# Forward row transform on sums and differences of the two image halves, with transposes, in a spectral convolution kernel

## What is computed

```python
    # layer 1
    m = jnp.mean(g, axis=(2, 3, 4), keepdims=True); s = jnp.var(...)   # _gn, groups of two channels
    x_ft = jnp.fft.rfft2(x)
    top = jnp.einsum('bixy,ioxy->boxy', x_ft[:, :, :m1, :m2], w1)      # m1 = m2 = 32
    bot = jnp.einsum('bixy,ioxy->boxy', x_ft[:, :, -m1:, :m2], w2)
    ...
    return jnp.fft.irfft2(out_ft, s=(h, w))
```

## Time and profile before

| | us |
|---|---|
| median of 3 runs | 2803.64 (2803.63 to 2803.73) |
| profiled execution | 2809.89 |
| its span (first to last instruction) | 2808.1 |
| PE busy in the span | 2221.9 (79%) |
| DVE busy | 1756.9 (63%) |
| ACT busy | 1290.3 (46%) |
| POOL busy | 554.7 (20%) |

### The profile page before, as it was taken

The page is one execution under the profiler, slowest core; times in us unless marked ns, Lnnn a source line. Parts: engine busy times, 40 slices in busy tenths (PEclk is TensorE's granted clock), DMA queues, the critical chain, the costliest instruction groups (busy, mean ns, idle before and its releaser), DMA issues. The chain is left out here.

```text
span 2808.1 us, 37222 instructions
## 1 busy us (share of the span) xinstructions
PE 2221.9 (79%) x15026; PEld 1346.0 (48%) x15026; DVE 1756.9 (63%) x1704; ACT 1290.3 (46%) x1562; POOL 554.7 (20%) x427
## 2 busy tenths in 40 slices
PE   0000089999999999998999999956676999888894
PEld 0000033333333333328999999955665555444452
DVE  8999889999999999992333333320001666545452
ACT  1111178889888898875445555510001222211110
POOL 1000024555333346330000000000100222111121
PEclk9999999999999999998999999988898999999997
DMA  9999869999999999978667777749998999999999
GB/s 403 431 430 418 320 219 342 342 340 347 332 335 347 335 347 343 340 247 325 234 256 258 263 254 264 265 135 388 395 395 320 372 417 417 418 417 417 418 417 387
DMA packets 419767, 958.23 MB, mean 341 GB/s; under 512 B 13888, under 2 KB 325744, under 8 KB 375312
## 3 DMA queue, kind: packets, MB, share of 16 engines
q1 hardware_dynamic: 230192, 593.46, 56.7%
q0 software_dynamic: 52176, 201.95, 18.0%
q10 hardware_dynamic: 137232, 160.45, 16.8%
HBM read 662.20 MB, written 293.60 MB: 340 GB/s over the span
## 5 line engine op out<-in xcount | busy, mean ns | idle before, releaser
L471 PE MATMUL psum<-mix_u,wcur 128*64 128x512 f32 x2048 | 881.9, 592 | 5.4 <-DVE mix_u L565 4.9
L471 PE MATMUL psum<-mix_v,wcur 128*64 128x512 f32 x2048 | 881.9, 592 | 0.0
L471 PEld LDWEIGHTS psum<-mix_u,wcur 128*64 128x64 f32 x2048 | 277.3, 136 | 596.1 <-issue 571.7
L1185 PE MATMUL psum<-tab_irow_icol,inv_t 128*128 128x512 f32 x1024 | 490.2, 602 | 50.0 <-ACT inv_t L1241 45.4
L1286 DVE TENSOR_TENSOR weights_or_rows<-weights_or_rows,psum 128x1024 f32<-128x1024 f32 x224 | 273.2, 1221 | 194.1 <-PE psum L1185 182.2
L1024 DVE COPY fwd_cols<-psum 128x544 f32<-128x544 f32 x128 | 141.8, 1108 | 396.8 <-PE psum L818 396.8
L818 PE MATMUL psum<-tab_frow_fcol_both_ident,fwd_x 128*128 128x128 f32 x3072 | 352.4, 276 | 4.2 <-DMA fwd_x<-x_scratch 4.2
L818 PEld LDWEIGHTS psum<-tab_frow_fcol_both_ident,fwd_x 128*128 128x128 f32 x3072 | 348.5, 193 | 5.5 <-DMA fwd_x<-x_scratch 4.3
L383 POOL COPY mix_v<-mix_u 64x2321 f32<-64x2321 f32 x128 | 339.4, 2652 | 26.6 <-PE psum L471 18.7
L729 DVE SCALAR_TENSOR_TENSOR tiles<-tiles 128x2048 f32<-128x2048 f32 x128 | 322.2, 2518 | 4.0
L510 ACT ACTIVATE tiles<-tiles,pcur 128x2048 f32<-128x2048 f32 x128 | 268.1, 2095 | 111.7 <-DVE tiles L729 105.1
(11 more groups left out here) (187 smaller groups left out, 1631.9 us busy)
## 6 DMA issues: line engine op xcount, KB each, us to landing
mix_u<-x SPq DMA_DIRECT2D x120, 1280.0 KB, 9.4
tiles<-x SPq DMA_DIRECT2D x64, 2048.0 KB, 12.4
x_scratch<-tiles ACTq DMA_DIRECT2D x128, 1024.0 KB, 9.2
weights_or_rows<-x_scratch SPq DMA_DIRECT2D x112, 1024.0 KB, 11.8
out<-weights_or_rows POOLq DMA_DIRECT2D x112, 1024.0 KB, 42.3
fwd_x<-x_scratch SPq DMA_DIRECT2D x96, 1024.0 KB, 6.8
x_tile<-x_scratch SPq DMA_DIRECT2D x46, 1024.0 KB, 9.0
weights_or_rows<-L_conv_w_real POOLq DMA_DIRECT2D x8, 4096.0 KB, 22.2
```

What stands on the lines that cost most here:

```text
L471: last = nc.tensor.matmul(bank(k * 4 + q, 512, C, e * C), wcur[j][:, e, m * C:(m + 1) * C], taps[e][:, r0:r0 + 2, m:m + W], start=(m == 0) ...
L1185: last = nc.tensor.matmul(bank(n % 2 * 2 + a), TS[n % 2][:, a * P:(a + 1) * P], icol, start=True, stop=True)
```

## The change

Rows 0 to 127 and 128 to 255 of the image are folded first. For an even mode the second half has the same table as the first, for an odd one the negated table. So the even modes need only the sum of the halves and the odd ones only the difference. `DVE` makes the sums (`sums_of`, 4 channels, 1024 elements), `POOL` the differences, each into four buffers. `frow` becomes two tables of 64 columns: cosines and sines of 17 even or 16 odd modes.

`rows(n)` now handles 2 channels, with the table as the stationary operand (64 columns) and the image as the moving one (512 columns); even modes go to partitions 0 to 63 and odd ones to 64 to 127 of one bank. The modes now lie on the partitions. ACT (even n) and DVE (odd n) copy a bank into `RS`, and PE turns it with four transposes of 128x128, so that the image column is on the partitions again. `turned` copies two such results at once with two DVE copies into `A`, which is laid out [column half a, parity, channel, 34]. Its innermost index is the mode, so `columns` reads its stationary operand with a stride of 34 floats. Four banks hold rows, two the transposes, and two are left for the columns (four before). ACT's squares share one scratch buffer, so each waits for the last. A tile's buffer is free again after sums, differences and squares, no longer after the rows. A step u of the new order handles 4 channels: two `rows`, two `transposes`. There are 16 steps per batch; column parts come after steps 1, 3, 5, 7 and 9.

```diff
-    frow = np.zeros((P, 2, P))
-    for half in range(2):
-        a = th * np.outer(np.arange(P) + half * P, np.arange(NM))
-        frow[:, half, :NM] = np.cos(a)
-        frow[:, half, NM2:NM2 + NM] = np.sin(a)
+    frow = np.zeros((P, 2, C))
+    for par in range(2):
+        k = np.arange(par, NM, 2)
+        a = th * np.outer(np.arange(P), k)
+        frow[:, par, :len(k)] = np.cos(a)
+        frow[:, par, NP:NP + len(k)] = np.sin(a)
...
-            A = [sb(ph, f"fwd_cols{i}", [P, 2, 4 * NP, C]) for i in range(2)]
+            ED = [[sb(ph, f"fwd_{n}{i}", [P, CG // 2, W]) for n in ("sum", "diff")] for i in range(NE)]
+            RS = [sb(ph, f"fwd_rows{i}", [P, 512]) for i in range(4)]
+            A = [sb(ph, f"fwd_cols{i}", [P, 2, 2, C, 2 * NP]) for i in range(2)]
...
-            junk = [sb(ph, f"fwd_junk{i}", [P, 2, 2 * W]) for i in range(2)]
+            junk = [sb(ph, f"fwd_junk{i}", [P, 2, 2 * W]) for i in range(1)]
...
+                    def rows(n):
+
+                        if n % 2 == 0:
+                            pe.wait_ge(sums_done, n // 2 + 1)
+                            pe.wait_ge(diff_done, n // 2 + 1)
+
+                        if n >= 4:
+                            pe.wait_ge(row_dve if n % 2 else row_act, (n - 4) // 2 + 1)
+                        for par in range(2):
+                            last = nc.tensor.matmul(bank(n % 4, 512, C, par * C), frow[:, par, :],
+                                                    ED[n // 2 % NE][par][:, n % 2 * 2:n % 2 * 2 + 2, :],
+                                                    start=True, stop=True)
                         last.then_inc(row_done, 1)
+
+                    def transposes(n):
+
+                        pe.wait_ge(row_dve if n % 2 else row_act, n // 2 + 1)
+                        if n == 0:
+                            pe.wait_ge(n2, 4)
+                        if n >= 2:
+                            pe.wait_ge(tr_out, n // 2 * 2)
+                        for q in range(4):
+                            at = (4 + n % 2) * 512 + q * P
+                            last = nc.tensor.transpose(psum[:, at:at + P], RS[n % 4][:, q * P:(q + 1) * P], ident)
+                        last.then_inc(tr_done, 1)
...
-                                mode = k * 2 * NP + 2 * p
                                 last = nc.tensor.matmul(
                                     psum[0:pair * C, at:at + P],
-                                    A[c % 2][:, a, mode:mode + pair, :].rearrange("p m c -> p (m c)"),
+                                    A[c % 2][:, a, 0:pair, :, k * NP + p].rearrange("p m c -> p (m c)"),
                                     fcol[:, a, k, :], start=(q == 0), stop=(q == 3))
...
+                    rows(0)
+                    rows(1)
+                    for u in range(NU_):
+                        c, g, second = u // 16 - 1, u % 16 // 2, u % 2 == 1
+                        if u + 1 < NU_:
+                            rows(2 * u + 2)
+                            rows(2 * u + 3)
+                        transposes(2 * u)
+                        transposes(2 * u + 1)
+                        if c >= 0 and g == 0 and not second:
+                            norm(c)
+                        if c >= 0 and second and g < PARTS:
+                            columns(c, g)
...
-                            if k >= 2:
-                                act.wait_ge(sq_done, k - 1)
-                            nc.scalar.activation(junk[g % 2][:, :, :],
+                            if k >= 1:
+                                act.wait_ge(sq_done, k)
+                            nc.scalar.activation(junk[0][:, :, :],
...
+                    def row_copy(n):
+
+                        dve.wait_ge(row_done, n + 1)
+                        if n >= 4:
+                            dve.wait_ge(tr_done, n - 3)
+                        v.tensor_copy(RS[n % 4][:, :], bank(n % 4)).then_inc(row_dve, 1)
+
+                    def turned(u):
+
+                        c, c0 = u // 16, u % 16 * 4
+                        if u % 16 == 0 and c >= 2:
+                            dve.wait_ge(col_done, (c - 1) * PARTS)
+                        dve.wait_ge(tr_done, 2 * u + 2)
+                        src = psum[:, 2048:3072].rearrange("p (c a r m) -> p c a r m", c=4, a=2, r=2)
+                        for a in range(2):
+                            dst = A[c % 2][:, a, :, c0:c0 + 4, :].rearrange("p r c m -> p c r m")
+                            last = v.tensor_copy(dst, src[:, :, a, :, 0:2 * NP])
+                        last.then_inc(tr_out, 2)
...
+                @block.gpsimd
+                def _(pool):
+                    for h in range(2 * B * NG):
+                        t = h // 2
+                        pool.wait_ge(loaded[t % NX], loaded_by(t))
+                        if h >= NE:
+                            pool.wait_ge(row_done, 2 * (h - NE) + 2)
+                        half = slice(h % 2 * CG // 2, (h % 2 + 1) * CG // 2)
+                        nc.gpsimd.tensor_tensor(ED[h % NE][1][:, :, :], XW[t % NX][:, 0, half, :],
+                                                XW[t % NX][:, 1, half, :], ALU.subtract).then_inc(diff_done, 1)
```

More of the change, by code:

```diff
@@ L765, in program @@
             recip_done = sem("norm2_recip")
-            RC = 4
-            NR = C // RC
+            NR = C // 2
+            NU_ = B * NR // 2
             GP = C // 2
@@ L852, in columns @@
                                 last = nc.tensor.matmul(
                                     psum[0:pair * C, at:at + P],
-                                    A[c % 2][:, a, mode:mode + pair, :].rearrange("p m c -> p (m c)"),
+                                    A[c % 2][:, a, 0:pair, :, k * NP + p].rearrange("p m c -> p (m c)"),
                                     fcol[:, a, k, :], start=(q == 0), stop=(q == 3))
                         last.then_inc(col_done, 1)
-                    for c in range(B):
-                        for n in range(NR):
-                            rows(c, n)
-                            if c == 0:
-                                continue
-                            if n == 0:
-                                norm(c - 1)
-                                columns(c - 1, 0)
-                            if n % 2 == 1 and n // 2 + 1 < PARTS:
-                                columns(c - 1, n // 2 + 1)
+                    rows(0)
@@ L893, in _, with squares @@
                 def _(act):
[L894 removed]
+                    def squares(t, half):
                         c = t // NG
[L897 to L900 removed]
+                        if half == 0:
+                            act.wait_ge(loaded[t % NX], loaded_by(t))
+                            if t % NG == 0 and c >= 2:
+                                act.wait_ge(spread_done, c - 1)
+                        for g in (2 * half, 2 * half + 1):
                             k = 4 * t + g
[L902 to L904 removed]
+                            if k >= 1:
+                                act.wait_ge(sq_done, k)
+                            nc.scalar.activation(junk[0][:, :, :],
                                                  XW[t % NX][:, :, 2 * g:2 * g + 2, :].rearrange("p a c w -> p a (c w)"),
@@ L1013, in finish @@
                                                 ALU.mult).then_inc(neg_done, 1)
[L1015 to L1038 removed]
+                    sums_of(0)
+                    sums_of(1)
+                    for u in range(NU_ + 1):
+                        c, at = u // 16 - 1, u % 16
+                        if u < NU_:
+                            row_copy(2 * u + 1)
+                            if c >= 0 and at == 0:
+                                spread(c)
+                        if u >= 1:
+                            turned(u - 1)
+                        if u + 2 < NU_:
+                            sums_of(u + 2)
+                        if c < 0 or u == NU_:
+                            continue
+                        if at == 1:
+                            variance(c)
+                        if at == 2:
+                            scales(c)
+                        if at in (5, 8, 10):
+                            copies(c, ON_DVE[(5, 8, 10).index(at)])
+                        if at == 11:
+                            finish(c)
                     spread(B - 1)
```

97 lines of the change are left out of this document (39 added, 58 removed).

## The result

| | median, us | runs | ratio to before (95%) |
|---|---|---|---|
| before | 2803.68 | 2803.63 to 2804.06 | |
| changed | 2913.26 | 2911.04 to 2916.30 | 1.0391 (1.0378 to 1.0404) |

The change costs 109.6 us, 3.9%. The forecast was 2852, so the side was right and the range (2735 to 2935) held the time, but the forecast of +48.5 was less than half of what came. The profiled execution took 2916.3 us, its span 2914.5.

A forecast was written before the change was run, and what follows sets the result against it. PE was taken to bound every step of the forward stage. Batch 0 -5.5, seven batches at +5.6 (+39.2) and the tail +14.8 gave +48.5, so a median of 2852 us, range 2735 to 2935.

The forecast's parts named there:

- PE work in a step: Forward rows: 4 matmul pairs at 0.43 plus eight transposes at 0.112, 2.62 us per 4-channel step where it was 3.58.
- Columns: the price of the stride: Column matmuls: strided weight load at 1.73 ns per column takes 221 ns and sets the pitch; 30.1 us a batch, not 15.2.
- Shared access: DVE's sum and POOL's difference exclude one another: eight steps per batch run at 3.4, not 2.62, adding 6.2 us.
- Batch 0: First batch, rows only: a first sum and difference, then 16 steps of 3.4 us: 57.7 where 63.2 stood, -5.5.
- Rival A: Column weight loads: the stride costs nothing; batch 63.3 us, total 2733 us, faster than before; chance 0.23.
- B: Column weight loads: each costs 464 ns, as L1159's median says; batch 111.2 us, total 3116 us; chance 0.06.
- the norm, copies and finish, some 5.4 us a batch, stay: DVE's other work per batch in the forward stage was taken as unchanged, some 5.4 us.
- The figure of 3.4: Shortest step with POOL always at work: sum 1.22, difference 2.1 and hand-overs 0.08 us, one after another.
- a first sum and difference ahead of any row, 3.3: Start of the first batch: 3.3 us for one sum and difference before rows begin.
- ACT, the turned copies, the loads: ACT 3.0 us a step, under 3.4; turned copies 0.44 each on DVE; loads at 308 GB/s with four tiles of lead.
- C: PE's clock falls to 1.2 GHz in the 72 steps at 3.4 us: +132, so 2984 us; chance 0.05.
- D: PE rows: matmul halves don't overlap or the ring of waits leaves PE idle: +164, so 3016 us; chance 0.06.

The follow-up runs named there:

- e1: Changed kernel, but the column matmuls read neighbouring floats of A instead of floats 136 B apart (wrong values, same work): 2778.7 us, ratio 0.9908 to before.
- e3: Changed kernel with A laid out mode, parity, channel, so stationary columns are neighbours, and copies run channel innermost: 2779.3 us, ratio 0.9910 to before.
- e4: Kernel before with only the changed kernel's layout of A and its copies; rows unfolded, POOL idle: 2939.7 us, ratio 1.0481 to before.
- e5: Changed kernel, but POOL forms differences of only two of four channels and odd matmuls read these twice: 2853.3 us, ratio 1.0180 to before.
- e9: Both edits of e6 and e7 together, on the layout of e3: 2784.3 us, ratio 0.9935 to before.
- e7: e3 with the 17 column pairs spread over steps 1 to 13, their copies, finish and store moved: 2795.6 us, ratio 0.9971 to before.
- e8: Changed kernel, columns reading A at strides from 1 to 34 floats in different blocks (wrong values); only pitches are read: 2890.1 us, one run.
- e6: e3 with spread and negation moved from DVE to ACT and the 64x1 addition made a tensor_scalar: 2751.2 us, ratio 0.9813 to before.

## Why the forecast was off

The range held the time and the two mechanisms were the right ones, but the forecast of +48.5 was 62.5 us short in the stage. Four terms were too small: PE's work in a step (7 x 4.3 = 30 us), the price of the columns (17), the shared access (9) and batch 0 (6).

- **PE work in a step**, 2.62, measured 2.89. The parts were right (pairs 0.43 apart, halves overlapping, transposes of one instruction each, 0.11 apart after a first gap of 0.165). What failed is the step "4 x 0.43 + 8 x 0.112": it has no term for changing between two kinds of matmul. The first pair takes 0.05 more, the way into the transposes 0.10, and eight transposes with the way back 1.02, not 0.90. +4.3 us a batch. What PE does at these seams no run shows.
- **Columns: the price of the stride**, 221 ns, measured 241 to 244. This was the largest term of the change, taken from DVE's price per element, and it was right in kind and 10% short: (341 - 80)/128 = 2.04 ns a column, not 1.73. e1, e3 and e4 give the term by itself: 134 to 136 us for the whole program. +2.1 us a batch, +2.6 in the tail (32.7 against 30.1). That DVE's price came so near was in part luck: no run says why it should hold for PE's load. Rival A (no price) and B (464 ns) are both refuted.
- **Shared access**, 6.2 us a batch, measured 7.5, and for another reason. The forecast let all eight steps without columns run at 3.4. The lone ones between two blocks run at 2.89, since the block gives DVE and POOL time to get ahead. The excess lies in the row of steps 11 to 0, and there mostly where DVE's helpers come. The forecast had "the norm, copies and finish, some 5.4 us a batch, stay": that is the step that failed, for two of them now wait for POOL's lock, 2.3 and 1.8 us in place of 0.15 and 0.2. That 6.2 came near 7.5 is luck in part, as some 2 us of the 7.5 are the clock's. This is an estimate: step 0 takes 4.4 us in four batches and 5.7 to 6.1 in the three with a spell at 1.2 GHz in it, and nine such spells fall into the seven batches. The figure of 3.4 was itself made of errors that cancel: POOL's difference takes 2.37 and not 2.1, but sum and difference together need 3.31 (batch 0's pace), not 1.21 + 2.37 = 3.58, so they overlap for some 0.3. The Trainium skill, GPSIMD Engine Reference, section 3.1, gives POOL 1.96 times DVE's time; the trace agrees, 1.21 x 1.96 = 2.37.
- **Batch 0**, 57.7, measured 63.7. Steps ran at 3.3 where 3.4 was forecast. What failed is "a first sum and difference ahead of any row, 3.3": PE's list has the rows of the next step ahead of the transposes of this one, so the first transposes wait for two differences and, at the lower clock, for 16 row instructions: 1283.7 - 1273.8 = 9.9 us. +6.0.
- **ACT, the turned copies, the loads** cost nothing, as argued: copies 0.426 (0.44 forecast), row copies 0.60 and 0.68.
- **C**, the lower clock in steps without columns, was wrong as put. Spells of 3.4 us at 1.2 GHz exist, ten in the stage, but behind stalls; e5 has the transposes without them. **D** fell with the pairs at 0.43 apart; the ring of waits cost nothing in steps whose sums came in time.

Sum: 7 x (4.3 + 2.1 + 1.3) + 6.0 + 2.6 = 62.5, and 48.5 + 62.5 = 111.0, against 110.4 measured in the stage.

So the fold itself is a gain (e3: -24 us, 0.9%, with the same idea and another layout), and the parity layout, whose copies are contiguous, pays 134 us for it at the matmul's weight load. The contiguous copies weren't even needed: e3's cost the same.

## What to carry to other kernels

Lay out a tile for the reader that has no slack: a weight load beside a 128-column matmul has none, while the copy that fills the tile can run over either index, and in runs of 16 B it costs no more than in long ones. When an idle POOL is given work, list DVE's small operations on SBUF, for each may now wait for a whole POOL instruction, and put none of them on the path to PE. When an order is moved, work out anew where each DMA lands: e9's expectation failed on that, and e7's in part.

## What the runs showed of the hardware

- A float32 weight load of 128 columns costs about 1.8 ns for each 16-byte piece of SBUF that it touches per partition, up to strides of 16 B, and it hides under 0.112 us of matmul (e8). Strides of 48 and 96 B are worse (262 and 247 ns) than 64 or 128 B (215, 217). Why is open.
- The exclusion of DVE and POOL hangs on the form: an addition of 64x1 with two SBUF tensors took 2.32 us beside POOL, with a per-partition scalar 0.20. A second SBUF input is not the only case: the copy L1037, from SBUF to SBUF, took 1.79 instead of 0.22.
- The weight load of a transpose took 140 ns (L835) where that of a matmul with as many columns took 192 (L818 of the kernel before), at nearly the same pitch.
- Issuing three stores held ACT's queue for 3.75 us in the place shown under e6, and for 1.94 in e9.
